# A selective-scan language-model block on one core: the first unit's work chain placed ahead, the rest of the opening placed inside units 0 to 2

## The reference, cut to what matters

```
h   = table[x][:, 192:256]                       # 2 x 2048 tokens, 64 wide
u   = layernorm(layernorm(h)) * ln_g + ln_b
act = silu(conv4(u @ in_w_x.T)); gate = silu(u @ in_w_z.T)
for d in (forward, backward over time):
    xr = silu(conv4(act @ in_w_x[d].T)); z = silu(act @ in_w_z[d].T)
    dt = softplus(xr @ xproj_dt.T @ dt_w.T + dt_b); B, C = xr @ xproj_BC.T
    s[t] = exp(dt[t] * A) * s[t-1] + dt[t] * xr[t] * B[t]     # 128 channels x 16 states
    y    = sum_n s * C + xr * D;  out[d] = (y * z) @ out_w[d].T
h = h + layernorm(h) + (concat(out) * silu(gate)) @ out_w.T
h = h + relu-MLP of the one best of 32 experts on layernorm(h)
```

## Time and profile before

| | |
|---|---|
| median of 3 runs | 606.04 us (605.75 to 606.38) |
| profiled execution, its own time | 607.73 us |
| span of the profiled execution | 605.9 us |
| busy: PE, DVE, ACT, POOL | 480.8, 483.3, 357.5, 517.9 us |
| first decay, first scan | 78.92, 83.44 us |

### The profile page before, as it was taken

One profiled execution on the slowest core, in us unless ns is written; L12 is line 12 of the kernel. 1 busy time (PEld: TensorE's weight loads), 2 busy tenths in 40 slices (PEclk: granted clock), 3 DMA queues, 4 the chain that ended last, 5 costly groups with the idle time before them and its releaser, 6 DMA issues.

```text
span 605.9 us, 5758 instructions
## 1 busy us (share of the span) xinstructions
PE 480.8 (79%) x1679; PEld 177.7 (29%) x1679; DVE 483.3 (80%) x601; ACT 357.5 (59%) x634; POOL 517.9 (85%) x190
## 2 busy tenths in 40 slices
PE   2576858777788888869888888878887887888897
PEld 1232212232323232314232323232333223323243
DVE  2533069998989896999899889988998899799941
ACT  2454565758585856483857485848574764354533
POOL 5737159999999999999999999999999999989600
PEclk9997958899999897998998999999999998789999
DMA  6839458855555546564644864386429741900000
GB/s 66 33 32 183 84 133 199 192 148 123 152 121 147 130 141 138 144 140 143 138 110 116 190 159 108 98 189 178 109 78 187 195 114 45 207 3 10 9 1 17
DMA packets 51073, 71.32 MB, mean 118 GB/s; under 512 B 16434, under 2 KB 17378, under 8 KB 51042
## 3 DMA queue, kind: packets, MB, share of 16 engines
q1 hardware_dynamic: 48050, 69.63, 47.6%
q0 software_dynamic: 1024, 1.05, 4.5%
q10 hardware_dynamic: 1968, 0.29, 0.3%
HBM read 60.45 MB, written 10.49 MB: 117 GB/s over the span
## 4 chain that ended last, share of the span: by engine, by line
POOL 33%; issue 26%; PE 18%; DVE 15%; ACT 5%; DMA 2%; POOLq 0%; DVEq 0%; ACTq 0%
POOL st L464 16%; POOL st L455 12%; DVE st L1350 9%; DVE st L1337 3%; PE ps L580 2%; PE ps L640 2%; PE ps L646 2%; POOL l_ L441 2%; POOL dt L444 2%; DMA x<-in_L_tok_ple_table,idx 2%; PE ps L627 2%; PE ps L732 2%; PE ps L748 2%; POOL x L429 1%; PE ps L568 1%
## 5 line engine op out<-in xcount | busy, mean ns | idle before, releaser
L464 POOL TENSOR_TENSOR st<-st,repC 128x2048 f32<-128x2048 f32 x63 | 284.9, 4533 | 9.1 <-ACT carry L998 7.8
L1350 DVE TENSOR_TENSOR_SCAN st<-ps,carry,st 128x512 f32<-128x512 f32 x192 | 234.9, 1268 | 19.6 <-ACT carry L998 12.9
L992 ACT ACTIVATE ps<-dtS,negA 128x512 f32<-128x512 f32 x256 | 169.5, 681 | 51.8 <-DVE st L1350 50.4
L455 POOL TENSOR_TENSOR st<-duS,repB 128x2048 f32<-128x2048 f32 x31 | 140.5, 4531 | 0.5 <-PE ps L646 0.5
L640 PE MATMUL ps<-Bw,nought 128*128 128x512 f32 x194 | 103.6, 645 | 0.0
L646 PE MATMUL ps<-st,fold 128*32 128x512 f32 x504 | 69.5, 624 | 42.9 <-POOL st L464 42.7
L1350 DVE TENSOR_TENSOR_SCAN st<-ps,zero,st 128x512 f32<-128x512 f32 x64 | 78.1, 1267 | 3.8 <-POOL st L455 1.9
L1337 DVE TENSOR_TENSOR st<-duS,ps 128x2048 f32<-128x2048 f32 x33 | 75.0, 2271 | 6.3 <-PE ps L627 6.3
L580 PE MATMUL ps<-act,wT 128*128 128x512 f32 x128 | 62.4, 633 | 5.2 <-ACT act L943 5.2
L998 ACT ACTIVATE carry<-st 128x4 f32<-128x4 f32 x48 | 9.8, 204 | 77.7 <-DVE st L1350 77.5
L640 PEld LDWEIGHTS ps<-Bw,nought 128*128 128x128 f32 x194 | 35.6, 202 | 50.0 <-issue 49.9
(11 more groups left out here) (129 smaller groups left out, 590.4 us busy)
## 6 DMA issues: line engine op xcount, KB each, us to landing
dtS<-dt_dram SPq DMA_DIRECT2D x64, 256.0 KB, 6.9
duS<-du_dram SPq DMA_DIRECT2D x64, 256.0 KB, 4.6
repC<-bc_dram SPq DMA_DIRECT2D x64, 256.0 KB, 5.7
repB<-bc_dram SPq DMA_DIRECT2D x60, 128.0 KB, 2.9
dt_dram<-dt SPq DMA_DIRECT2D x16, 256.0 KB, 2.1
du_dram<-du SPq DMA_DIRECT2D x16, 256.0 KB, 2.0
bc_dram<-bc_sb SPq DMA_DIRECT2D x16, 64.0 KB, 5.5
out_h<-fin SPq DMA_DIRECT2D x8, 128.0 KB, 2.0
```

Source lines behind the costliest of these rows:

```text
L455: pool.tensor_tensor(st[:, r], duS[:, u % 2], row, ALU.mult).then_inc(sem("dbu_pool"), 1)
L464: pool.tensor_tensor(st[:, r], st[:, r], row, ALU.mult).then_inc(sem("hc_ready"), 1)
L992: sc.activation(decay_bank(u, r, q), dtS[:, u % 2, q], ACT.Exp, scale=negA[:, way(u), q, r:r + 1]).then_inc(sem("decay_ready"), 1)
L1350: dve.tensor_tensor_scan(st[:, r, q, order], decay_bank(u, r, q)[:, order], st[:, r, q, order], first, ALU.mult, ALU.add).then_inc(sem("sc ...
```

## The change

On POOL, all 32 gathers and the constants come first, `softplus(0)` is gone from it, and `softplus(1)` and `softplus(2)` stand in unit 0. DVE finishes the first softplus (`first_softplus`) and makes all four input products of unit 0, the first of them in four pieces of 512 columns (`first_product`), each ahead of its scan. SP loads `dt` and `du` of unit 0 in the same four pieces, each with a semaphore of its own, drops the loads of B for unit 0, and issues the expert weights (`late_loads`) after unit 1's loads and not ahead of everything. The norm has two sets of buffers (`xc`, `lnr`, the statistics in PSUM), so two chunks' norms overlap. PE turns all weights early and does only chunk 0 and chunk 1 before the first scan. The act of chunks 2 and 3 and the convolutions of units 2 and 3 are done inside unit 0, and ACT loads its tables twice there; z of units 1 and 2 and the gates of chunks 1 and 2 go into unit 1's burst, z of units 3 and 4 and the gate of chunk 3 into unit 2's, z of units 5 and 6 into unit 3's. Chunks 4 to 7 are normed one unit later, in units 1 to 5. PE gets matmuls of zeros in the opening: five of `write_nought` into a free bank and three of `add_nought`. Left out of the diff below are the renamed norm helpers, waits that only follow the new order, and places of staging buffers.

```diff
     def on_dve(u):
         if u == 0:
-            return (0, 1, 3)
+            return (0, 1, 2, 3)
         return (1, 2, 3) if u in () else (1, 3)
...
     def norm_a(u):
-        if 0 <= u < CB:
-            return CB + u
+        if 1 <= u <= CB:
+            return CB + u - 1
...
+        def zeds(u):
+
+            return {1: (1, 2), 2: (3, 4), 3: (5, 6)}.get(u, (u + 3,) if u + 3 < UNITS else ())
...
+            def four_times(of, u, q):
+
+                return of[u][32 * q:32 * q + 32].unsqueeze(0).broadcast_to([4, 32, T])
+
+            def first_loads_of(q):
+
+                sp.wait_ge(sem("dt_in_dram"), 16)
+                sp.dma_start(dtS[:, 0, q, :], four_times(dt_dram, 0, q)).then_inc(sem(f"dt_first_{q}"), 16)
+                sp.wait_ge(sem("du_in_dram"), 16)
+                sp.dma_start(duS[:, 0, q, :], four_times(du_dram, 0, q)).then_inc(sem(f"du_first_{q}"), 16)
...
                 sp.dma_start(to, fin[:]).then_inc(sem("out_done"), 16)
 
-            for u in range(2):
-                store_bc(u)
-                store_dt(u)
-                store_du(u)
-                load_dt(u)
-                load_du(u)
-                load_B(u)
-                load_C(u)
+            store_bc(0)
+            store_dt(0)
+            store_du(0)
+            for q in range(NQ):
+                first_loads_of(q)
+            load_C(0)
+            store_bc(1)
+            store_dt(1)
+            store_du(1)
+            load_du(1)
+            load_B(1)
+            load_dt(1)
+            load_C(1)
+            with nc.allow_non_contiguous_dma(reason="b1 is 2 KB"):
+                for dst, src in late_loads:
+                    sp.dma_start(dst, src).then_inc(sem("late_in"), 16)
...
-            for t in range(TB, TB + 5):
-                gather(t)
-            softplus(0)
-            for t in range(TB + 5, TILES):
+            for t in range(TB, TILES):
                 gather(t)
...
-            softplus(1)
-            pool.wait_ge(sem("constants_ready"), 1)
             for u in range(UNITS):
                 if u:
                     by_c(u - 1, NR - 1)
+                if u == 0:
+                    softplus(1)
                 if 2 in on_pool(u):
                     input_product(u, 2)
                 by_c(u, 0)
-                if u + 2 < UNITS:
+                if 2 < u + 2 < UNITS:
                     softplus(u + 2)
                 by_c(u, 1)
                 if u + 1 < UNITS:
                     input_product(u + 1, 0)
                 by_c(u, 2)
+                if u == 0:
+                    softplus(2)
...
             def gate_chunk(n, bank):
-                if bank == LONG:
-                    pe.wait_ge(sem("act_ready"), n + 1)
-                wait(pe, "gate_ready", n)
+                if n == 0:
+                    pe.wait_ge(sem("wT_copied"), 7)
+                elif n == 1:
+                    pe.wait_ge(sem("x_ready"), 4)
+                else:
+                    pe.wait_ge(sem("act_ready"), CB + 1 if n == CB - 1 else n + 1)
...
-            def zed(u, bank):
+            def zed(u, bank, at):
+                wait(pe, "z_ready", u)
+                if u == 0:
+                    pe.wait_ge(sem("act_ready"), 4)
+                    pe.wait_ge(sem("wT_late"), 1)
                 if bank == ZED:
...
+
+            def write_nought(n, bank):
+
+                for _ in range(n):
+                    pe.matmul(ps[:, bank, :], nought[:], nought[:].unsqueeze(1).broadcast_to([P, TC, P]),
+                              start=True, stop=True)
...
             dt_weights(0, 7)
+            way_b_weights()
+            write_nought(1, 0)
             turn_chunk(0)
+            dt_weights(1, 9)
+            write_nought(1, 0)
             x_chunk(0, 1)
-            gate_chunk(0, 0)
-            turn_chunk(1)
+            write_nought(1, 0)
             conv(0, 1)
             pre(0)
             bc(0)
-            way_b_weights()
+            write_nought(2, 0)
+            turn_chunk(1)
+            gate_chunk(0, 0)
+            b_rows(0, 0)
             x_chunk(1, 1)
-            gate_chunk(1, 0)
             turn_chunk(2)
-            dt_weights(1, 9)
             conv(1, 2)
-            zed(0, 3)
-            zed(1, 3)
-            x_chunk(2, 1)
-            gate_chunk(2, 0)
-            conv(2, 2)
-            zed(2, 3)
-            turn_chunk(3)
             pre(1)
             bc(1)
-            x_chunk(3, 1)
-            gate_chunk(3, 0)
-            pe.wait_ge(sem("constants_ready"), 1)
-            b_rows(0, 0)
-            for u in range(UNITS):
+            turn_chunk(3)
+            skip_product(0)
+            add_nought(3)
+            b_rows(0, 1)
+            x_chunk(2, LONG)
+            b_rows(0, 2)
+            x_chunk(3, ZED)
+            conv(2, PRE)
+            b_rows(0, 3)
+            sum_states(0, 0)
+            zed(0, ZED, 0)
+            conv(3, LONG)
+            pre(2)
+            sum_states(0, 1)
+            bc(2)
+            for u in range(1, UNITS):
                 second, third = u - 1 in ENDS, u - 2 in ENDS
                 if u + 2 < UNITS:
                     pre(u + 2)
...
-                if u + 3 < UNITS:
-                    zed(u + 3, ZED)
-                if 1 <= u <= CB:
-                    gate_chunk(CB + u - 1, LONG)
+                for v in zeds(u):
+                    zed(v, ZED, u)
+                    if u < 3 and v % 2 == 1:
+                        gate_chunk((v + 1) // 2 if u == 1 else 3, LONG)
+                    elif u == 1:
+                        gate_chunk(2, LONG)
+                if 2 <= u <= CB + 1:
+                    gate_chunk(CB + u - 2, LONG)
...
             sc.wait_ge(sem("dtproj_ps"), 1)
             out_of_psum(dtproj[:, 0, :], ps[:, PRE, 2 * P:3 * P], "dtproj_ready")
             decay_rates(0)
+            sc.wait_ge(sem("wT_ps"), 6)
+            out_of_psum(dt_wT[:, 1], ps[0:R, 2, P:2 * P])
+            out_of_psum(wT[:, 15, 2 * NS:4 * NS], ps[:, 2, 0:2 * NS])
             uT_chunk(0)
-            squares(1)
-            rsqrt(1)
             silu_tables()
             act_silu(0, 1)
-            gate_silu(0, 0)
-            uT_chunk(1)
+            sc.wait_ge(sem("dtproj_ps"), 2)
+            out_of_psum(dtproj[:, 1, :], ps[:, 2, 2 * P:3 * P], "dtproj_ready")
+            squares(1)
             conv_silu(0, 1)
             exp_ln_tables()
+            squares(2)
+            rsqrt(1)
             softplus_in(0)
             softplus_exp(0)
             softplus_plus1(0)
             softplus_ln(0)
+            rsqrt(2)
             bc_out(0)
-            squares(2)
-            rsqrt(2)
-            sc.wait_ge(sem("wT_ps"), 6)
-            out_of_psum(dt_wT[:, 1], ps[0:R, 2, P:2 * P])
-            out_of_psum(wT[:, 15, 2 * NS:4 * NS], ps[:, 2, 0:2 * NS])
             decay_rates(1)
+            uT_chunk(1)
+            silu_tables()
+            gate_silu(0, 0)
+            act_silu(1, 1)
             uT_chunk(2)
             squares(3)
+            conv_silu(1, 2)
+            exp_ln_tables()
             rsqrt(3)
-            sc.wait_ge(sem("dtproj_ps"), 2)
-            out_of_psum(dtproj[:, 1, :], ps[:, 2, 2 * P:3 * P], "dtproj_ready")
-            silu_tables()
-            act_silu(1, 1)
-            gate_silu(1, 0)
-            z_silu(0, 3)
-            conv_silu(1, 2)
-            z_silu(1, 3)
-            act_silu(2, 1)
-            gate_silu(2, 0)
-            conv_silu(2, 2)
-            z_silu(2, 3)
-            uT_chunk(3)
-            act_silu(3, 1)
-            gate_silu(3, 0)
-            exp_ln_tables()
-            softplus_in(1)
-            softplus_exp(1)
-            softplus_plus1(1)
-            softplus_ln(1)
-            bc_out(1)
-            sc.wait_ge(sem("constants_ready"), 1)
-            sc.wait_ge(sem("gate_ready"), CB)
-            for u in range(UNITS):
...
+            def first_unit(p):
+
+                if p == 1:
+                    softplus_in(1)
+                    bc_out(1)
+                if p == 2:
+                    softplus_exp(1)
+                    softplus_plus1(1)
+                if p == 3:
+                    softplus_ln(1)
+                    uT_chunk(3)
+                if p == 5:
+                    keep_last(0, 0)
+                if p == 6:
+                    silu_tables()
+                    act_silu(2, LONG)
+                    act_silu(3, ZED)
+                    exp_ln_tables()
+                if p == 9:
+                    keep_last(0, 1)
+                if p == 11:
+                    silu_tables()
+                    conv_silu(2, PRE)
+                    z_silu(0, ZED)
+                    conv_silu(3, LONG)
+                    exp_ln_tables()
+                if p == 13:
+                    keep_last(0, 2)
+                    softplus_in(2)
+                if p == 14:
+                    softplus_exp(2)
+                    softplus_plus1(2)
+                if p == 15:
```

(102 more changed lines are left out.)

227 lines of the change are left out of this document (117 added, 110 removed).

## The result

The changed kernel took 710.36 us (median of 4, 708.86 to 711.76) against 606.21 us (4 runs, 605.75 to 606.40): ratio 1.172 (1.169 to 1.175). The forecast was 585 us. It is 125 us off, and on the wrong side.

A forecast was written before the change was run, and what follows sets the result against it. After the opening POOL's list of work was taken to bound the kernel, so an earlier start moves the end: -25.6 + 1.6 (slips in the chain) + 3.0 (bursts) = -21.0 us, 606.0 to 585.0 us; range 577 to 594.

The forecast's parts named there:

- The loads: Unit 0's dt and du, 2 MB at 184 GB/s: 11.4 us, first pair at 44 to 46, last about 53.
- The stores: Opening: SP stores dt and du, each taking 2 us to land, and loads du's first quarter from 41.3 us.
- Rival A: Unit 0's loads stand behind the gathers: last pair about 64, scan 3 at 66, 7 us later, 592; chance 11%.
- Unit 0: DVE's list after the first decay sums to 33.0 us, ACT's to 28.8; first scan of unit 1 at 84.2.
- The table loads: Four ACT table loads in unit 0 take 5.1 us, without the extra drain of about 1.38 us per switch.
- Rival B: PE at the lower clock level in unit 0, and longer bursts: 8 + 2 us, 593 to 595; chance 12%.
- The bursts: Ends of units 1 to 3, longer by 1.7, 2.6 and 1.2 us: 3.0 us given back, bounds 0 and 6.
- The margin of 2.1 us: In unit 4 DVE ends scan 3 2.1 us before POOL takes its rows; 4.5 us of delay then costs 2.4.
- rival D: Nothing is given back in the bursts and POOL keeps its lead: 581, or 577 with a faster chain; chance 10%.
- The zeros: Matmuls of zeros keep PE at work from about 14 us, so the upper clock level was taken from 24 us.
- rival C: The zeros don't raise PE's clock; 0.94 us a matmul until unit 1, 24 of 25.6 us gone, 607; chance 4%.
- the anchor: POOL's product with C of unit 0's last rows, by_c(0, 3): from 113.7 to 88.1 us, a gain of 25.6.

The follow-up runs named there:

- the run with the gathers held: the base, with POOL issuing the last 11 gathers only when du is in DRAM: 604.51 us, ratio 0.995.
- the base: Changed kernel with units 1 to 15 loading dt and du in the old form, each unit 0 quarter as four 32-row transfers: 610.3 us, ratio 1.003.
- the run with all three: the base with the last 11 gathers held, rank and pick copied before the first product, and the old kernel's later burst order: 595.45 us, ratio 0.981.
- the bursts alone: the base with early silus back in the opening or unit 0 and later bursts as in the kernel before: 593.51 us, ratio 0.976.
- the gathers in three: the base with gathers issued in three groups, rank and pick copied behind unit 0's third scan, old later burst order: 595.67 us, ratio 0.972.
- the later loads mended: Changed kernel with dt and du of units 1 to 15 again loaded as four transfers of 32 partitions: 620.77 us, ratio 1.024.

## Why the prediction was wrong

**The loads (failed, +90 us in units 1 to 15, +10 us in unit 0).** The working took the new transfers at "the 184 GB/s that unit 0's window moved", a rate of the old form, and it priced the new form for unit 0 alone; of unit 1's loads it said they "have from 60.6 to 74 us". The changed form stands in `load_dt` and `load_du` too, for all of units 1 to 15, and its rate is 100 GB/s. 2 MB then take 21 us. With C's rows among them, the loads issued from 165.20 us on held the decay at 193.10, 28 us later, and since they start only when a buffer of `du` is free, the units came 38 us apart for POOL's 31. No bound covered this, since nothing had been put down for it: "everything else is hidden". In unit 0, which the working did price, the third of the four first products still waited 6.61 us for its quarter of `du` and started at 72.88 us, where the last pair was to be there at "about 53".

**The stores (failed, +6 us).** "SP stores each (2 us to land)". 2.0 us is right without gathers in flight (measured with them held) and 9.4 with them; the earlier trace rows had 8.3 and 8.6 us for transfers that met gathers, and I applied them to loads only. "ACT, not these loads, sets the first decay" held for ACT (49.0 for 48.8) and failed for the loads. Rival A, the loads among the gathers, is what then happened once the store was early, in the run with the gathers held: scan 3 started at 64.4 and ended at 65.6 (A: 66, forecast 59.3), and the first scan of unit 1 came at 91.25 for 84.2, so its 7 us are the right size. So the two stand on top of each other.

**Unit 0 (half right).** The list of DVE was right in its terms except one, the copy of `rank`: 4.2 us, where the working had 0.6 for it and `pick` together. In the base the first scan of unit 1 stood at 93.17 for 84.2: 6 us from the first decay, 4 from the copy, and some that DVE made up. The table loads were as the trace before had them: 1.28 us, the next activation 1.29 us later, no drain. Rival B, PE at the lower level in unit 0, didn't happen: the x chunks of unit 0 in the base took 1.88 us and the convolutions 3.60, and the granted clock from 54 to 93 us was 0.85 for the 0.72 of before.

**The bursts (right mechanism, wrong size).** 3.0 us, bounds 0 and 6; measured in the base 15.6 - 3.6 = 12.0 us between units 1 and 7, twice the upper bound. The slips were seen one by one, but PE stands in each of them: its z waits for ACT to clear the bank, its sums, its softplus projection and its rows for r = 1 stand behind that z in its order, and DVE, ACT and POOL wait for these in turn. The margin of 2.1 us, taken once, was spent in every unit up to 5, as POOL's wait of 4.41 us in unit 4 shows. With bursts as before they are 0 in the run with all three, which was rival D's case and needed another order; the traces of the bursts alone and of the gathers in three, each from the longest execution of its kernel, still lose 5.3 and 5.4 us behind unit 1.

**The zeros.** PE's conv(0) took 3.70 us in the changed kernel and x_chunk 1.99, the short lengths that the forecast took, so rival C didn't happen. That the zeros did it isn't shown. Without them the time was the same within 0.4% in two pairs, but both pairs stood on the chip with the stall, where the first x chunk was long with and without zeros (3.70 to 3.78 us in all four); conv(0) took 3.60 us in both kernels with zeros and 3.70 and 5.97 us without, with no time lost in the end. And in the kernel with the gathers in three, an opening without the stall and with the zeros, it took 3.59 us, for 1.99 in the run with all three. The granted clock doesn't tell long from short chunks: it is 1.00 in the windows around all of them (22 to 30 us, and 34 to 46 us where the stall moved them). The working took the length of a matmul here and the granted clock of 0.72 in the old unit 0 for signs of one and the same lower level, which these rows don't bear out.

**The balance.** The changed kernel's ratio 1.172 is 1.024 with the later loads mended, 1.003 with the quarters mended, 0.976 with the bursts too, and 0.972 at best. The net gain of 21 us that was forecast is there for about four fifths (0.972 is 17 us), in a kernel in which these faults are mended; of the 25.6 us at the anchor some 15 are there as POOL's lead. That this comes near 585 says nothing for the prediction, which was for the changed kernel.

## What to carry to other kernels

When a diff rewrites a transfer "into the same buffer", read the outermost dimension of its source and price it for every unit in which the line runs, before looking at the order; a rate is a row of one form of transfer and doesn't pass to another. A lead won in an opening is worth only what the later stages' tightest cycle lets through, so work moved out of the opening must not land in the stage where ACT and PE hand one bank to and fro. And where a chain of small stores and loads runs beside a long train of gathers, cut the train at the places where the chain needs the DMA engines: it was worth 6 and 8 us in the two pairs on chips with the stall, by a shorter or absent stall. On a chip without it the store landed 7 us sooner, but only 1.9 us of that reached unit 1.

## What the runs showed of the hardware

A transfer whose source begins with a run of 4 kept four packets under way at every moment (100 GB/s), with a run of 2 two (51 GB/s), and the old form, with a run of 32, mostly 16 or more (230 GB/s from 84 to 94 us). A copy of int32 to float32 (128x32) on DVE took 0.17 or 0.18 us when POOL ran nothing, and otherwise ended with the POOL step of its time: 4.22, 4.21, 2.43 and 1.55 us beside products, 0.74 to 0.76 us beside a step of the softplus. A store of 256 KB landed in 2.0 us on quiet queues and in 8.1 to 10.6 us amid gathers. ACT can stand still in a stretch full of gathers, for up to 14.4 us at a time and 16 us in two stops, with no releaser in the trace, on two of the four chips used for experiments; the same kernel was 595.45 us on one chip and 608.34 us on another, while the kernel before moved from 607.7 to 610.0.
